# Taking the last of 1601 keys off all others, so that 64 keys are left over for the half tile

## The reference, cut to what matters

```python
q = (x @ Wq)...; k = (context @ Wk)...; v = (context @ Wv)...
sim = jnp.einsum('bhid,bhjd->bhij', q, k) * SCALE      # 1601 keys j
attn = jax.nn.softmax(sim, axis=-1)
out = jnp.einsum('bhij,bhjd->bhid', attn, v)
x = x + out.transpose(0, 2, 1, 3).reshape(B, Nq, HEADS * DIM_HEAD) @ Wo + bo
```

## Time and profile before

| | |
|---|---|
| median of 3 runs | 3302.86 us (3302.56 to 3302.99) |
| the profiled execution, its own time | 3302.1 us |
| its span, first to last instruction | 3300.3 us |
| PE busy | 3269.1 us (99%) |
| PE weight loads busy | 2606.8 us (79%) |
| DVE, ACT, POOL busy | 2383.1 us (72%), 1938.2 us (59%), 1069.6 us (32%) |
| mean granted TensorE clock | 0.998 |

### The profile page before, as it was taken

The page is one execution under the profiler, slowest core; times in us unless marked ns, Lnnn a source line. Parts: engine busy times, 40 slices in busy tenths (PEclk is TensorE's granted clock), DMA queues, the critical chain, the costliest instruction groups (busy, mean ns, idle before and its releaser), DMA issues.

```text
span 3300.3 us, 40940 instructions
## 1 busy us (share of the span) xinstructions
PE 3269.1 (99%) x15518; PEld 2606.8 (79%) x15518; DVE 2383.1 (72%) x4915; ACT 1938.2 (59%) x2236; POOL 1069.6 (32%) x710
## 2 busy tenths in 40 slices
PE   8999999999999999999999999999999999999999
PEld 6777777777787777877777777777777877777887
DVE  6777777777777777777777777777777777777655
ACT  4565555655556555665556655566655666575554
POOL 4322233222332233322233222322223322225555
PEclk9999999999999999999999999999999999999999
DMA  2000000000000000000000000000000001000000
GB/s 79 1 16 1 16 1 11 6 1 16 1 16 1 16 1 16 1 1 16 1 16 1 16 1 16 1 9 8 1 16 1 16 1 39 1 3 4 7 7 10
DMA packets 8055, 32.39 MB, mean 10 GB/s; under 512 B 1585, under 2 KB 2354, under 8 KB 7474
## 3 DMA queue, kind: packets, MB, share of 16 engines
q1 hardware_dynamic: 7858, 29.78, 2.9%
HBM read 27.41 MB, written 2.10 MB: 9 GB/s over the span
## 4 chain that ended last, share of the span: by engine, by line
PE 98%; DVE 1%; issue 0%; ACT 0%; DMA 0%; POOL 0%; POOLq 0%; DVEq 0%; ACTq 0%
PE st L529 12%; PE st L532 12%; PE st L535 12%; PE op L543 12%; PE op L549 12%; PE op L546 12%; PE side L475 11%; PE side L555 3%; PE st L636 2%; PE st L638 2%; PE st L637 2%; PE side L468 1%; PE side L470 1%; PE side L469 1%; PE op L636 1%; PE op L637 1%
## 5 line engine op out<-in xcount | busy, mean ns | idle before, releaser
L796 ACT ACTIVATE p_full<-st 128x1024 f32<-128x1024 f32 (+1 forms) x832 | 853.8, 1026 | 1128.5 <-PE st L535 1128.4
L1061 DVE TENSOR_REDUCE m_part<-side 128x1 f32<-128x402 f32 x2016 | 1078.2, 571 | 550.6 <-PE side L475 550.6
L410 POOL TENSOR_TENSOR p_lo<-p_full,p_hi 128x1024 fp32r<-128x1024 f32 x256 | 669.2, 2614 | 2063.7 <-ACT p_hi L799 2063.7
L799 ACT ACTIVATE p_hi<-st 128x1024 fp32r<-128x1024 f32 (+1 forms) x832 | 848.6, 1020 | 0.0
L1049 DVE TENSOR_TENSOR p_lo<-p_full,p_hi 128x1024 fp32r<-128x1024 f32 (+1 forms) x576 | 700.3, 1216 | 132.7 <-ACT p_hi L799 132.7
L475 PE MATMUL side<-cT_hi,qT_hi 96*128 96x402 f32 x2016 | 555.2, 346 | 0.0
L529 PE MATMUL st<-qT_hi,cT_hi 97*128 97x512 f32 (+1 forms) x1664 | 538.4, 405 | 2.3 <-DMA qT_hi<-m_row 2.3
L543 PE MATMUL op<-p_hi,v_hi 128*97 128x512 f32 (+1 forms) x1664 | 527.1, 398 | 0.5 <-DVE p_lo L1049 0.5
L532 PE MATMUL st<-qT_lo,cT_hi 96*128 96x512 f32 (+1 forms) x1664 | 524.8, 397 | 0.0
L535 PE MATMUL st<-qT_hi,cT_lo 96*128 96x512 f32 (+1 forms) x1664 | 521.9, 395 | 0.0
L549 PE MATMUL op<-p_hi,v_lo 128*97 128x512 f32 (+1 forms) x1664 | 521.1, 394 | 0.0
(11 more groups left out here) (164 smaller groups left out, 2606.0 us busy)
## 6 DMA issues: line engine op xcount, KB each, us to landing
keys_nat<-in_ctx_keys SPq DMA_DIRECT2D x16, 624.0 KB, 5.8
keys_tur<-in_ctx_turned SPq DMA_DIRECT2D x16, 603.0 KB, 4.9
gud_raw<-in_moe_w SPq DMA_DIRECT2D x2, 1152.0 KB, 7.8
out_x<-x SPq DMA_DIRECT2D x8, 256.0 KB, 2.0
x<-in_x SPq DMA_DIRECT2D x1, 1920.0 KB, 12.1
qT_hi<-m_row SPq DMA_DIRECT2D x64, 4.0 KB
aw<-in_attn_w SPq DMA_DIRECT2D x2, 448.0 KB, 5.3
aw<-in_attn_w SPq DMA_DIRECT2D x1, 896.0 KB, 9.3
```

Source lines behind the costliest of these rows:

```text
L410: pool.tensor_tensor(p_lo[:, slot(s), :], p_full[:, s % 2, :], p_hi[:, slot(s), :].bitcast(F32), ALU.subtract).then_inc(s_lo_pool, 1)
L796: act.activation(p_full[0:m, s % 2, :], both(st[0:m, s % 2]), ACT.Exp, scale=SCALE)
L799: act.activation(p_hi[0:m, slot(s), :], both(st[0:m, s % 2]), ACT.Exp, scale=SCALE).then_inc(s_ex, 1)
L1061: dve.tensor_reduce(m_part[:, at:at + 1], where[:, 0:MAXW], AX.X, ALU.max).then_inc(s_drain, 1)
```

## The change

The last key c1600 of a batch is subtracted from all its other keys. Softmax does not change when all scores lose the score of the last key; the score of the last key is then 0 and its probability exp(0 - maximum). The values lose c1600 too, which is put back by adding c1600 B, summed over the heads, plus the bias. Left are 1600 keys: twelve tiles and one half tile of 64.

- The half tile holds the 64 keys' high parts in columns 0 to 63 and their low parts in 64 to 127. `scores(12)` is four matmuls (two passes), with the sum of two partition halves still to be made: ACT copies the low half out of PSUM (`low_half`), DVE adds the high half (`sum_half`) into `s_half`, and the exponentials of step 12 read that. `lo(12)` writes the low part of the probabilities beside the high part, and `weigh_half` is four matmuls.
- `scores(0)` of the next group waits for `sum_half` where it waited for the exponentials of step 12.
- ACT's order at the end of a group: `low_half`, the two Q, the exponentials of step 12, `keep_last`. DVE's: `lo(11)`, `sum_half`, two Q, `lo(12)`.
- The places of the side jobs: Y moves from steps 8, 11, 11, 11 to 4, 6, 8, 10; T to the front of step 11's `weigh`; QQ to before `weigh(10)`; N from step 6 to 7; a new job U (c1600 times the sum of B, and bias) in step 5 of one group in four. M takes 400 columns for 402.
- `add_head` adds the last key's exponential to the denominator (one more small DVE operation); `keep_last` makes these exponentials on ACT, once a group.
- POOL subtracts the last key from a piece of the next batch's keys (`piece_shifted`, after step 3, two operations); for batch 0 it does so at once before it splits it.
- At the end of group 0 DVE sums B over the heads. The loops' arithmetic for semaphore counts is rewritten with one running number; the counts mean the same.

```diff
+    NC = KEYS - 1
-        PLACES = {2: ("MM", "M"), 3: ("MM", "M"), 4: ("MM", "MM"), 5: ("MM", "M"), 6: ("MM", "MM"),
-                  7: ("MM", "MM"), 8: ("MM", "MY"), 9: ("MM", "MM"), 10: ("MM", "MM"), 11: ("YY", "YT"),
-                  12: ("", "QQ")}
-        EXTRA = {2: {5: "L", 6: "N"}, 3: {5: "R"}}
+        PLACES = {2: ("MM", "M"), 3: ("MM", "M"), 4: ("MM", "MMY"), 5: ("MM", "M"), 6: ("MM", "MMY"),
+                  7: ("MM", "MM"), 8: ("MM", "MY"), 9: ("MM", "MM"), 10: ("MM", "MMY"), 11: ("T", ""),
+                  12: ("QQ", "")}
+        EXTRA = {1: {5: "U"}, 2: {5: "L", 7: "N"}, 3: {5: "R"}}
+        def places(g):
+            drop = {0: "Y", NG - 2: "LQ", NG - 1: "MTQ"}.get(g, "")
...
@@ gpsimd
+            def shift(cols, tiles):
+                n = tiles.stop - tiles.start
+                pool.tensor_scalar(keys_tur[:, cols], keys_tur[:, cols], keys_tur[:, NC:KEYS], None, ALU.subtract)
+                return pool.tensor_tensor(keys_nat[:, tiles, :], keys_nat[:, tiles, :],
+                                          keys_nat[:, S:S + 1, :].to_broadcast([P, n, DC]), ALU.subtract)
             pool.wait_ge(s_nat, 16)
-            pool.tensor_copy(v_hi[0][:, :, 0:DC], keys_nat[:, :, :]).then_inc(s_sh, 1)
             pool.wait_ge(s_ch, 1)
-            pool.tensor_tensor(cT_lo[0][:, :], keys_tur[:, :], cT_hi[0][0:DC, :].bitcast(F32), ALU.subtract)
+            shift(slice(0, NC), slice(0, S)).then_inc(s_ss, 1)
+            pool.wait_ge(s_ss, 1)
+            pool.tensor_copy(v_hi[0][:, :, 0:DC], keys_nat[:, 0:S, :]).then_inc(s_sh, 1)
             pool.wait_ge(s_sh, 1)
+            split_lo(0, slice(0, NC), slice(0, S)).then_inc(s_v, NGB)
...
+                    if b < B - 1 and s < 9:
+                        {3: piece_shifted, 5: piece_hi, 7: piece_lo}[s](b, i, g)
@@ tensor
+            def taken_off(where, batch):
+                pe.matmul(where[:, 0:D], last_T[:, batch:batch + 1].to_broadcast([OW, P]), B_sum[:, :],
+                          start=True, stop=True).then_inc(s_fill, 1)
                 for j in range(2):
-                    pe.matmul(st[0:m, s % 2, j, :], cT_hi[par][0:DC, keys], qT_lo[slot][:, halves[j]],
-                              start=False, stop=False)
-                for j in range(2):
-                    mm = pe.matmul(st[0:m, s % 2, j, :], cT_lo[par][:, keys], qT_hi[slot][0:DC, halves[j]],
+                    mm = pe.matmul(st[:, s % 2, j, :], cT_hi[par][0:DC, keys], qT_lo[slot][:, halves[j]],
+                                   start=False, stop=(s == FULL))
+                for j in range(2 if s < FULL else 0):
+                    mm = pe.matmul(st[:, s % 2, j, :], cT_lo[par][:, keys], qT_hi[slot][0:DC, halves[j]],
                                    start=False, stop=True)
...
+            def weigh_half(par):
                 for j in range(2):
+                    pe.matmul(op[0:OW, j, :], v_lo[par][0:TAIL, FULL, :], p_hi[0:TAIL, slot(FULL), halves[j]],
                               start=False, stop=False)
                 for j in range(2):
+                    mm = pe.matmul(op[0:OW, j, :], v_hi[par][:, FULL, :], p_hi[:, slot(FULL), halves[j]],
+                                   start=False, stop=True)
                 mm.then_inc(s_pv, 1)
...
-                        pe.wait_ge(s_drain, jobs + (j - 1))
+                        pe.wait_ge(s_drain, j - 1)
...
-                pe.wait_ge(s_ex, n + S)
+                pe.wait_ge(s_sum, g + 1)
@@ scalar
+                def low_half():
+                    act.wait_ge(s_qk, n + S)
+                    act.activation(s_half[:, :], both(st[TAIL:P, FULL % 2]), ACT.Copy).then_inc(s_low, 1)
...
+                low_half()
                 for k, j in enumerate(place["Q"]):
-                    queries_hi(bank(first_bank + j), jobs + (j + 1), k, i % 2)
+                    queries_hi(bank(j), j + 1, k, i % 2)
+                exp(FULL)
+                if g < NG - 1:
+                    if g:
+                        act.wait_ge(s_drain, place["Y"][-1] + 1)
+                    keep_last(g + 1)
@@ vector
+                dve.tensor_tensor(whole[:, :].rearrange("p (q y) -> p q y", q=2), ys[:, :, D:YW], last,
+                                  ALU.add).then_inc(s_rc, 1)
...
+                def sum_half():
+                    dve.wait_ge(s_low, g + 1)
+                    dve.tensor_tensor(s_half[:, :], both(st[0:TAIL, FULL % 2]), s_half[:, :],
+                                      ALU.add).then_inc(s_sum, 1)
...
                 for t in range(2, S):
-                    side_jobs(at[t][0])
-                    lo(t - 1)
                     if t == S - 1:
+                        lo(t - 1)
+                        sum_half()
+                        side_jobs(at[t][0])
                         lo(t)
+                    else:
+                        side_jobs(at[t][0])
+                        lo(t - 1)
                     side_jobs(at[t][1])
```

More of the change, by code:

```diff
@@ L45, in xattn_moe @@
     OW = DC + 1
+    assert TAIL == P // 2 and NC % 4 == 0
     stack = ExitStack()
@@ L214, in job_at @@
[L214 to L225, removed]
+        order = ["".join(a + b for a, b in places(g).values()) for g in range(NG)]
@@ L227, in turns, with jobs_at @@
+        first_job = [JOBS0 + sum(len(o) for o in order[:g]) for g in range(NG + 1)]
+        JOBS_END = first_job[NG]
+        def jobs_at(g):
+            return {kind: [first_job[g] + j for j, o in enumerate(order[g]) if o == kind] for kind in KINDS}
         def turns(body):
[L229 to L232, removed]
+            for b in range(B):
+                for i in range(NGB):
+                    body(b, i, b * NGB + i)
@@ L298, in body @@
                     load_moe_weights(2, 10, 16)
-                if last and i == NGB - 1:
+                if g == NG - 1:
                     sp.wait_ge(s_qk, (NG - 1) * S)
@@ L498, in _ @@
                 for j in range(2):
[L499 removed]
+                    tile, part = u % (NT), u // (NT) * 2 + j
                     mm = pe.matmul(where[:, j, 0:MAXW], qT_hi[0][0:DC, tile * P:(tile + 1) * P],
@@ L599, in pv @@
                 def pv(s):
-                    if s == 0:
-                        pe.wait_ge(s_oe, bb * (2 * NGB) + (g + 1))
-                    wait_rest(pe, bb, g, s)
-                    weigh(s, par)
-                at = places(i, last)
+                    if s == 0 and g:
+                        pe.wait_ge(s_oe, g)
+                    wait_rest(pe, g, s)
+                    if s < FULL:
+                        weigh(s, par)
+                    else:
+                        weigh_half(par)
+                at = places(g)
                 for t in range(2, S):
@@ L766, in _, with keep_last @@
             act.wait_ge(s_sel, 1)
-            act.wait_ge(s_set, 1)
+            def keep_last(group):
+                act.wait_ge(s_mc, group + 1)
+                act.activation(e_last[:, group % 2, :], m_neg[:, :].bitcast(F32), ACT.Exp, scale=SCALE).then_inc(s_el, 1)
             def keep_output(steps):
-                act.wait_ge(s_pv, steps + 1)
+                act.wait_ge(s_pv, steps)
                 act.activation(oT[:, :], both(op[0:OW]), ACT.Copy).then_inc(s_oe, 1)
+            keep_last(0)
             def weights_hi(q):
@@ L802, in body @@
                 exp(0)
-                keep_output(n)
-                for s in range(1, S):
+                if g:
+                    keep_output(n)
+                for s in range(1, FULL):
                     exp(s)
-                    if last and i == 2 and 1 <= s <= 9:
+                    if g == NG - 2 and 1 <= s <= 9:
                         weights_hi(s - 1)
-                    elif last and i == 3 and 2 <= s <= 9:
+                    elif g == NG - 1 and 2 <= s <= 9:
                         weights_hi(s + 7)
-                    elif last and i == 3 and s == 1:
+                    elif g == NG - 1 and s == 1:
@@ L935, in add_head, with add_taken_off @@
                 ins.then_inc(s_drain, 1)
+            def add_taken_off(where, filled, tiles):
+                dve.wait_ge(s_fill, filled)
+                plus = where[:, 0:D].rearrange("p (t d) -> p t d", t=1).to_broadcast([P, 2, D])
+                dve.tensor_tensor(x1[:, tiles, :], plus, x1[:, tiles, :], ALU.add).then_inc(s_drain, 1)
             one = lambda t: t.rearrange("p t (g a) -> p t g a", a=1)
@@ L1010, in _ @@
                 where = (st[:, 0], st[:, 1], op)[u % 3]
-                tile, part = u % (NM // 4), u // (NM // 4) * 2
+                tile, part = u % (NT), u // (NT) * 2
                 if u == NM // 2 - 2:
@@ L1015, in _ @@
                 dve.wait_ge(s_mx, u + 1)
-                dve.tensor_reduce(m_part[:, tile * 4 + part:tile * 4 + part + 2], where[:, :, 0:MAXW], AX.X,
+                dve.tensor_reduce(m_part[:, tile, part:part + 2], where[:, :, 0:MAXW], AX.X,
                                   ALU.max).then_inc(s_mxd, 1)
@@ L1031, in weights_lo, with body @@
```

(20 more changed lines are left out.)

361 lines of the change are left out of this document (193 added, 168 removed).

## The result

The changed kernel took 3432.84 us (median of 4 runs, 3431.94 to 3433.25) against 3302.71 us before: a ratio of 1.0396 with a 95% interval of 1.0378 to 1.0414, 130 us slower. 3418 us was forecast, with a range of 3345 to 3470.

The account below looks back on a forecast made before the run. PE was taken to bound the kernel, its list gapless. From 3302.1 us, -59.6 - 1.7 + 136 + 6 + 5 + 5 + 19 + 1 + 2 + 3 = +115.7 gave 3418 us, own range 3370 to 3460, widened to 3345 to 3470.

Parts of the forecast that it names:

- What bounds the kernel: PE's list, busy 99% without gaps: work removed comes off, and waits put in are added, at full price.
- Y behind two Ms: Steps 4, 6 and 10: Y waits for DVE's reduce of the first M, 186 x 0.73 = 136 us added (89 to 153).
- Passes taken out: Half tile: two matmuls of scores and two of outputs fewer in each of 64 groups, 59.6 us off.
- N one step later: Step 7: N still behind two Ms, with a `lo` on DVE ahead of them, 6 us added (0 to 20).
- U, re-entry: New job U 16 x 0.3 = 5 us; Y and T in five separate places of a group, 5 us (0 to 10).
- The end of a group: `weigh_half` waits for `lo(12)` behind the longer ACT and DVE chain: 0.3 us x 63 = 19 us (0 to 55).
- The head: Start of the run: POOL's subtraction and batch 1's loads delay the maxima row, 3 us added (0 to 7).
- DVE's sum of B: After group 0: 2048 elements, 2.4 us on DVE, break the next group's fit once, 1 us added.
- The last group: With nothing behind it, the longer chain at the group's end shows in full, 2 us added.
- the bank is free in time: Rival: Y behind two Ms waits for nothing, run faster at 3282 or 3263 us; chance 0.07.
- a smaller stall: Rival: PE's list takes up part of Y's wait, 56 us for 136, 3339 us, still slower; chance 0.08.
- the group's end is what grows: Rival: `low_half` or `sum_half` meets a busy engine, `lo(12)` wait 1 us or more a group, 3465 to 3500; chance 0.09.

Follow-up runs that it names:

- experiments 1 and 2: 1: changed kernel, side-job table with one M before Y for two, 3297.55 us; 2: kernel before with the changed kernel's side-job places, QQ staying, 3446.67 us.
- the reverse edit: seven with the half tile's third passes of scores and outputs put back, on other data: 3310.3 us, 51.5 us more than seven.
- Experiment 3: Changed kernel with the first two matmuls of `weigh_half` over 128 rows for 64: 3420.92 us.
- experiment 4: Changed kernel with the maxima row sent before the loads of batch 1 in SP's head: 3425.14 us.
- experiment 5: Changed kernel with `weigh_half` moved after both scores of the next group: 3426.28 us.
- seven: Changed kernel with one M before Y, `weigh_half` over all rows and after both scores, maxima row first, N in step 8: 3258.79 us.

## Why the prediction was right, step by step

The mechanism and its place were right, and the sign hung on them; several sizes were off.

- *What bounds the kernel.* PE's list was gapless; the waits put into it were added. Shown by experiments 1 and 2 from both sides, 135 and 145 us.
- *Y behind two Ms.* Forecast 186 x 0.73 = 136, measured 186 times and 0.75, 140. The 0.14 us for two more weight loads, its upper bound, is shown by no run: Y's stall is 0.07 above N's 0.68. The evidence was one job, N, that already stood in that place sixteen times.
- *Passes taken out.* Forecast 59.6, measured 51.5 as the reverse edit with what it covers. The count of matmuls fell by 240, as forecast, but by luck: it is 256 less the 32 of U (two a time, where one was counted) and 16 more of the four Ys that group 0 no longer has.
- *N one step later.* Forecast 6. The wait of N's loads went from 13.1 us to 18.4, 5.3 us.
- *U, re-entry.* U is 2 x 16 matmuls, 0.22 us each time in the timeline, 3.5 for 5. The re-entries were put at 5 and cost nothing: from start to start four Ys and T cost 1.89 us a group before (MY 0.44, YY 0.89, YT 0.55) and 4.13 after (three MMY of 1.19, MY 0.44, T 0.11), and without three stalls of 0.75 that is 1.88.
- *The end of a group.* The term that was mis-sized most: 19 forecast, 0.48 x 63 = 30 measured. The chain of ACT and DVE came out within 0.1 us. What failed is the sentence "what follows is the same work": `weigh_half` was priced as two ordinary pairs. Experiment 3 shows 0.17 us a group for the change of rows; without it 0.31 are left, the 0.3 of the forecast. That "two pairs" had gone ahead of zero was a slip (it is one pair, two matmuls) on which nothing hung.
- *The head.* Forecast 3, measured 5.9 in the trace. The choice in the middle of 0 to 7 was a choice without a row. The Trainium skill's rule ("DMA: Bandwidth & Descriptors", "Queues, rings and completion order": on each DMA engine the descriptors of one queue are consumed in ring order) was put at 6; by that rule, the trace agrees, with 5.6 us from issue to use behind the loads and 2.0 ahead of them (experiment 4). That the 6 was met so closely is part luck: the two subtractions on POOL took 4.33 and 2.86 us for 3.4 and 2.7, and the split ended at 37.7 for 36.3.
- *DVE's sum of B*: 3.91 us for the 2.4 taken from `lo`, and PE idle for 2.1 us ahead of `weigh(0)` for 1.

```profile
91.34 3.91 DVE L1191 TENSOR_REDUCE B_sum<-B_all 96x128 f32<-96x2048 f32 x1
...
96.53 0.79 PE L570 MATMUL op<-p_hi,v_hi 128*97 128x512 f32 x2 [2.07 <-DVE p_lo L1119]
```

The forecast had only the wait. Behind it the granted clock stands at 0.50, the 1.2 GHz level, from 97.0 to 100.4 us, and a pair takes 0.85 us from start to start for 0.465. This group takes 51.2 us where others of its kind take 47.4: 3.8 us, of which 1.6 are the clock's.

- *The last group.* Forecast 2 us. At both its ends the queries (QQ, 1.41 us of PE's time), which elsewhere stand beside the longer chain, are missing, and `weigh_half` waits 1.48 us at 3054.72 and 2.86 at 3095.67, where the kernel before waited 0.49 once; behind each wait the granted clock stands at 0.50 again for 3.4 us. In all this costs 7.5 us more than before.

The sum by measured sizes: -60.5 (passes, and 1 for the Ms' columns) + 139.5 + 5 + 3.5 + 28.5 (the ends of 61 groups) + 6 (head) + 4 (sum of B) + 7.5 (last group) - 2 (group 0 without its Ys) = 131.5, and the spans differ by 131.1 (3431.4 to 3300.3). The forecast's 115.7 lacks 16: the row count in `weigh_half` (10), the last group (5), the stall, the head and the sum of B (3 each), less the re-entry (5) and other small terms.

A group was forecast at 47.2 us and takes 47.66 (`weigh_half` at 1526.98 and again at 1574.64). The rivals: "the bank is free in time" and "a smaller stall" fell with the first row of the waits and its 0.75 us; "the group's end is what grows" fell too: the wait for `lo(12)` is 0.23 us a group, not 1, and `sum_half` met no busy engine. The end did grow, by 11 us more than forecast, but through the row count, which no rival had.

## What to carry to other kernels

Where the bounding engine's list has no gap, a change that removes work from it is worth that work, less the waits that the work had covered, and one wait put in at the wrong place undoes it: here three Ys behind two Ms each cost more than twice what the passes gave. Before moving a job, look for one that already stands in such a place and read its wait from the trace. With two buffers in turn and a reader slower than the jobs (here 0.57 us for 0.19), the third job in a row waits for the first one's reader, as it did in every one of the 186 and 189 places here; put longer work of another kind between, and look also at what the reading engine has of its own in that step.

## What the runs showed of the hardware

- A pair of matmuls over 64 rows between ones over 96 to 128 rows keeps the next weights from being loaded under it: the weight load sits idle for 0.37 us on the way in and 0.39 on the way out, and in experiment 5, where no wait lies over it, three pairs take 0.56, 0.63 and 0.55 us for 0.465, 0.35 us in all. With all 128 rows in the same place (seven) they take 0.47, 0.46 and 0.47. With 65 rows there was none of that: pairs with 65 rows followed each other at 0.465. The Trainium skill has it in words, "TensorEngine Tiling (Array Packing)", "Key Properties": changing the tiling mode, as against the tile, drains TensorE. That fits what is seen here, and I had not weighed it; that 64 rows put the array into another mode is inferred from the vanished gap, no row names a mode.
- After each of three waits in which PE had been idle for 1.48, 2.07 and 2.86 us its granted clock fell from 1.00 to 0.50 (the 1.2 GHz level), at which a pair of 512 columns took 0.85 us for 0.465. It stood at 1.00 through the waits for Y, 0.48 us idle each.
- A DVE sum over a strided view (16 heads innermost, 2048 elements) took 1.9 ns an element, a contiguous two-operand subtraction 1.2 ns (1216 for 1024).
- On POOL, subtracting a per-partition value took 4.33 us for 1600 columns where a subtraction of two tensors took 3.43 for 1536: 2.7 to 2.2 ns a column. I had put it at the latter.
